# Where the row-maxima chunks stand in the pure attention steps of a fused convolution and attention kernel

## What is computed

```
f1 = w1 @ xf + b1;  f2 = w2 @ xf + b2;  f3 = w3 @ xf + b3      # xf: 32 x 4096 per image
A = softmax(einsum('bcn,bcm->bnm', f1, f2), axis=-1)           # 4096 x 4096 scores per image
out = einsum('bcm,bnm->bcn', f3, A) + xf
```

## Time and profile before

| | |
|---|---|
| median of 3 runs | 1299.03 us |
| profiled execution, span from first to last instruction | 1557.5 us |
| TensorE busy, its share of the span | 1255.7 us, 81% |
| VectorE busy | 993.9 us, 64% |
| ScalarE busy | 662.7 us, 43% |
| GpSimd busy | 485.1 us, 31% |
| mean granted TensorE clock | 0.875 of 2.4 GHz |

### The profile page before, as it was taken

The page is one execution under the profiler, slowest core; times in us unless marked ns, Lnnn a source line. Parts: engine busy times, 40 slices in busy tenths (PEclk is TensorE's granted clock), DMA queues, the critical chain, the costliest instruction groups (busy, mean ns, idle before and its releaser), DMA issues.

```text
span 1557.5 us, 20328 instructions
## 1 busy us (share of the span) xinstructions
PE 1255.7 (81%) x7126; PEld 508.6 (33%) x7126; DVE 993.9 (64%) x1679; ACT 662.7 (43%) x882; POOL 485.1 (31%) x537
## 2 busy tenths in 40 slices
PE   5999977387879888672587767876889999999996
PEld 1888843143423333220122222222222222222221
DVE  5899988253635544463464647665687777777772
ACT  5777766243424433111032322332346544444444
POOL 6000000746464565474655354654400000000000
PEclk9999978688988988755587779888999999999999
DMA  2655401543332331111111111111000000000000
GB/s 55 156 121 119 105 1 55 170 124 104 100 99 94 100 104 36 34 44 34 44 36 36 28 39 30 40 37 30 29 0 1 0 1 14 1 0 0 0 0 14
DMA packets 59672, 79.21 MB, mean 51 GB/s; under 512 B 12230, under 2 KB 43974, under 8 KB 59414
## 3 DMA queue, kind: packets, MB, share of 16 engines
q1 hardware_dynamic: 44342, 47.03, 11.6%
q0 software_dynamic: 15264, 31.29, 7.1%
HBM read 70.94 MB, written 7.34 MB: 50 GB/s over the span
## 4 chain that ended last, share of the span: by engine, by line
PE 58%; DVE 16%; another core or an unknown queue 12%; issue 9%; ACT 3%; SPq 1%; DVEq 1%; DMA 0%; ACTq 0%
PE psum L1971 11%; PE psum L1833 9%; PE psum L1953 9%; PE psum L1994 7%; PE psum L1718 5%; DVE maxes L1144 4%; DVE probs_and_weighted L881 3%; PE psum L1733 3%; PE psum L1668 2%; PE psum L1916 2%; PE psum L1745 2%; PE psum L1843 1%; PE psum L2000 1%; PE psum L1805 1%
## 5 line engine op out<-in xcount | busy, mean ns | idle before, releaser
L554 POOL DMA_INDIRECT tile_data<-quad_table,index_u x477 | 461.4, 967 | 626.0 <-DMA quad_table<-quad_rows_or_splits 245.2
L1144 DVE TENSOR_REDUCE maxes<-psum 128x1 f32<-128x512 f32 x512 | 331.1, 683 | 172.7 <-PE psum L1953 108.5
L1574 ACT ACTIVATE quads<-psum 128x1024 f32<-128x1024 f32 x256 | 248.2, 1021 | 329.8 <-PE psum L2000 214.8
L1971 PE MATMUL psum<-quads 128*64 128x512 f32 x1024 | 277.1, 637 | 0.0
L1833 PE MATMUL psum<-scratch,quad_rows_or_splits 128*128 128x512 f32 (+1 forms) x486 | 233.8, 626 | 33.2 <-DVE scratch L966 23.4
L1953 PE MATMUL psum<-products_or_attention 128*128 128x512 bf16 x256 | 101.5, 452 | 134.4 <-DVE maxes L1144 123.3
L1994 PE MATMUL psum<-quads,probs_and_weighted 32*128 32x512 f32 x1024 | 159.8, 696 | 2.6 <-ACT quads L1574 1.8
L1833 PEld LDWEIGHTS psum<-scratch,quad_rows_or_splits 128*128 128x128 f32 x486 | 96.3, 211 | 146.6 <-issue 126.4
L978 DVE TENSOR_TENSOR probs_and_weighted<-psum,quads 128x512 f32<-128x512 f32 (+1 forms) x81 | 50.6, 640 | 145.6 <-remote 80.2
L1433 ACT ACTIVATE vals<-psum 96x384 f32<-96x384 f32 x53 | 25.8, 487 | 222.9 <-remote 96.6
L1953 PEld LDWEIGHTS psum<-products_or_attention 128*128 (+1 forms) x256 | 20.8, 99 | 266.4 <-DVE maxes L1144 176.3
(11 more groups left out here) (227 smaller groups left out, 1464.9 us busy)
## 6 DMA issues: line engine op xcount, KB each, us to landing
products_or_attention<-positions SPq DMA_DIRECT2D x30, 576.0 KB, 8.2
products_or_attention<-bands SPq DMA_DIRECT2D x12, 768.0 KB
tile_data<-quad_table,index_u POOLq DMA_INDIRECT x477
quads<-bands SPq DMA_DIRECT2D x6, 768.0 KB
quad_table<-quad_rows_or_splits SPq DMA_DIRECT2D x4, 768.0 KB, 5.6
products_or_attention<-bands SPq DMA_DIRECT2D x4, 576.0 KB
quad_table<-quad_rows_or_splits SPq DMA_DIRECT2D x2, 640.0 KB, 7.3
products_or_attention<-positions SPq DMA_DIRECT2D x4, 288.0 KB, 7.0
```

The costliest lines, as they stand in the source:

```text
L554: pool.indirect_dma_start(out=out[:, k * CORNERS * C:(k + 1) * CORNERS * C], out_offset=None, in_=table, in_offset=bass.IndirectOffsetOnAx ...
L1144: v.reduce_max(maxes[:, tile_of_q, block_of_k:block_of_k + 1], psum[:, FREE + c % 2, :], AXIS_X)\
L1574: act.activation(probs[:, s % 2, 2 * BLK * h:2 * BLK * (h + 1)], psum[:, SCORES + 2 * h:SCORES + 2 * h + 2, :].rearrange("p a n -> p (a n) ...
L1971: last = pe.matmul(psum[2 * C * h:2 * C * h + 2 * C, SUMS, :], f3[b][:, 4 * s + i, :], probs[:, s % 2, BLK * i:BLK * i + BLK], start=s == ...
```

## The change

Two lines. The table of chunks a step becomes 6, 6, 4, 4, 4, 4, 4, 0 (32 chunks as before), and a step with 4 chunks has no group between the halves of the products: its 4 chunks stand as 2, 0, 2. A step with 6 stands as 2, 2, 2 by the formula that was there. No other table has a step with 4 chunks. No instruction is added or taken away.

```
-SCORED = [4, 5, 5, 5, 5, 4, 4, 0]
+SCORED = [6, 6, 4, 4, 4, 4, 4, 0]
...
                     ready = min(m, 2)
-                    half_way = ready if tiles and s % 2 == 0 else max(ready, m // 2 + ready // 2)
+                    half_way = ready if m == 4 or tiles and s % 2 == 0 else max(ready, m // 2 + ready // 2)
                     cuts = [c, c + ready, c + half_way, c + m]
```

## The result

The changed kernel takes 1289.81 us (median of 6 runs, 1286.77 to 1293.01) against 1300.37 us for the kernel before (6 runs, the three shown above among them). The ratio is 0.9919, with a 95% interval of 0.9903 to 0.9935: 0.8% faster, 10.6 us. The forecast was 10.4.

A forecast was written before the change was run, and what follows sets the result against it. TensorE's own sequence was taken to bound the attention blocks. Savings of -8.2 (image 1, blocks 0 to 5), -0.9 (its block 6) and -1.3 (image 0's block 6) gave -10.4 us: 1299.0 to 1288.6 us, range 1285 to 1296.

The forecast's parts named there:

- The bound: Attention-only blocks of image 1: TensorE, busy 37.0 of 37.8 us, sets the pace, so only its sequence or waits matter.
- The groups' cost: TensorE's steps: a middle group that goes frees 0.27 us (0.16 for splitting the halves, 0.11 for opening a group).
- the term -1.33 a block: TensorE's work per block: steps 5 and 6 -0.54, steps 2 to 4 -1.44, step 0 +0.43, step 1 +0.22 us.
- Block 6 of image 0: Attention block ahead of image 1: net -1.33 us, a fill covering the turn's delay and no stall in step 4.
- Rival 3: TensorE's groups cost nothing real, the 0.27 us being a recording effect: +0.2 us, a time of 1299; chance 0.06.
- Step 4's wait: Image 1's blocks 0 to 5: wait for VectorE's maxima behind a fill falls from 0.63 to 0.17 us, -0.46 each.
- The turn: Between image 1's blocks: step 6 ends with a pair, so VectorE's chain ahead of the transposition ends later, +0.39 us each.
- Rival 4: At the turn, the chain finds slack and costs nothing: 2.7 us more saved, 1286; chance 0.10.
- The sum: Image 1's blocks 0 to 5 -1.36 us each, its block 6 -0.90, image 0's block 6 -1.33: -10.4 us.
- Rival 1: VectorE's queue: paired maxima bring step 4's kind of wait to other steps, 1302, or 1296 with half; chance 0.12.
- Rival 2: TensorE's clock falls at its waits, chiefly the turn, at least 1.3 us an episode: 1298 or 1305.5; chance 0.06.
- block 0 of image 1: First block of image 1, counted at -1.36 us like blocks 1 to 5, its 1.2 GHz stretch read beforehand.

## Why the prediction was right

- **The bound.** TensorE's sequence sets the pace: 37.0 of 37.8 us before, 35.8 of 36.4 after. Every experiment that shortened it or a wait in it shortened the distance between turns.
- **The groups' cost.** The new step is 4.23 us against 4.22, and the term -1.33 a block stands. Block 6 of image 0, with no turn to pay for, saved 46.07 - 44.73 = 1.34. Its steps 2 to 6 show the cost free of waits: 1.94 less where 1.44 + 0.54 = 1.98 were worked out. Its steps 0 and 1 took 0.60 more against 0.65, but they stand in waits for VectorE in both kernels (0.54 and 1.02 in TensorE's timeline before; 0.54, 0.21, 0.81 and 0.21 after), so that agreement is partly luck. The split of 0.27 into 0.16 and 0.11 is shown by the kernel with split halves (37.09 against 37.1). Rival 3, that the groups cost nothing real, is out.
- **Step 4's wait.** 0.16 is left of 0.63; forecast 0.17.
- **The turn.** 0.49 behind the products; the term +0.39 stands (4.22 against 3.84, and the gap 0.49 against 0.10), and it is shown to come from the pair of maxima and the operation behind it, since either of two edits there takes it away. Rival 4, a chain with slack, is out.
- **The sum.** Image 1's blocks 2 to 5 save 1.35 to 1.40 each (forecast 1.36), its block 6 saves 0.87 (0.90).
- **Rival 1**, waits in other steps: none in steps 2, 3 and 5 of the block shown.
- **Rival 2**, the clock: in the turns, with a gap of 0.49, it stayed at 1.00 in every block of the windows above. By the Trainium skill's passage on cycling through PSUM banks (TensorE: Matmul & The Clock Gate, "A second HAM failure mode: psum-queue depth-cycling") the time should have come out slower; the trace doesn't bear that out at the turns.

What I missed is block 0 of image 1. It saved 2.85 and not 1.36, as the change's profile has no stretch at 1.2 GHz there. The prediction had read that stretch before, and took it to stay as it was. From the memset L1119 to the end the profiles give 395.97 - 383.97 = 12.0 us, and 10.4 forecast plus 1.5 there account for that. The medians' difference is 10.6, and the interval (8.5 to 12.6 us) holds both. So the timed runs can't tell a gain with this part from one without it, and that the forecast came within 0.2 us of them is luck; what the distances between turns confirm is the terms of the sum.

## What to carry to other kernels

Where TensorE is full, read start-to-start times of the same matmuls in different neighbourhoods: what a change of form costs (here 0.27 us for one group between the halves) is counted as busy time, so that no busy share shows it, and regrouping saves it with the same instructions. Ask next who consumes the regrouped results at the end of a phase: a pair in place of single ones delays the last consumer, here by 0.39 us, and moving an unrelated operation of the consumer into the gap that the regrouping opened took that back. Compare variants by the distance between two fixed points of each iteration: here it came out the same to 0.01 or 0.02 us in two profiles of one kernel (0.05 in block 0 of image 1), where single runs scatter by 6 (1286.77 to 1293.01).

## What was not expected of the hardware

- TensorE's clock as image 1 begins: behind the same sequence and the same wait of 0.84 us it fell to 1.2 GHz in one kernel and stayed at 2.4 GHz in another. Where it stays high, block 0 is 2.37 us longer than the later blocks (38.82 against 36.45). Against that, and this is an estimate, the low clock added 0.8 us (39.51 with the old cut in step 6) to 3.2 us (41.13 with the negated maxima first).
- After TensorE has waited at the transposition, the scores start 0.57 us behind it (1138.88 - 1138.31; in the kernel before, behind a gap of only 0.10, 1406.06 - 1405.48 = 0.58), and without a wait 0.32 (1138.34 - 1138.02, in the kernel with the negated maxima first): the turn lost 0.74 (4.22 - 3.48) with a gap of 0.49. What the other 0.25 is, no run here tells.
- The first profile of the kernel before had a span of 1557.5 us, its second 1298.6, with the last 396 us the same to 0.11.
